# Splitting the first eight tile loads between the SyncE and ScalarE DMA queues in a cross-attention kernel

## The chip, the cores and the metric

One core of one Trainium2 chip. The metric is the device time of one launch in microseconds (us), as the median over several executions; a profiled execution gives the trace.

## The reference

Thirty-two sequences, each with 512 tokens of `x` and 512 tokens of a context, 512 features in float32, go through one cross-attention layer with 16 heads of 32 features:

```python
def layer_norm(x, gamma, beta, eps=1e-05):
    mu = jnp.mean(x, axis=-1, keepdims=True)
    var = jnp.var(x, axis=-1, keepdims=True)
    return (x - mu) * jax.lax.rsqrt(var + eps) * gamma + beta
qn = layer_norm(q, q_norm_g, q_norm_b)          # q is x
kvn = layer_norm(kv, kv_norm_g, kv_norm_b)      # kv is the context
Q, K, V = qn @ Wq, kvn @ Wk, kvn @ Wv           # split into 16 heads
attn = softmax(Q K^T / sqrt(32))
out = q + gelu((attn @ V) @ Wo + bo)            # exact gelu
```

## The kernel before

**Work.** A token tile is 128 tokens by 512 features in float32 (256 KB). A batch is one sequence: four tiles of `x` (tiles 0 to 3) and four of the context (tiles 4 to 7), all kept in the buffer `tok`. A batch is computed in four steps of four heads each. TensorE makes the products; to keep float32 precision from the fast float32r products, most operands are split into a high part (written by ScalarE) and a low part (written by VectorE), and three products of parts are summed. VectorE finds the row maxima of the scores, ScalarE takes the exponentials, GpSimd adds the probabilities up. The order of the work on each engine is written out by hand in the table `ORDER`, and the engines are held together by semaphores. The loop runs the batches -1 (which only prepares batch 0), 0, 1 to 30 in a hardware loop, 31 and 32 (which only finishes batch 31).

**The head of the kernel**, on which the change bears, is batch -1:

- SyncE (SP) issues eight tile loads of batch 0 with `load_tile` (L387 to L392), then the four weights Wq, Wk, Wv, Wo of 1 MB each into `probs` (L385), and after that the copies of the stacked operands (L353), which wait for VectorE. Later it loads the tiles of each next batch and the residuals, and stores the result.
- ScalarE (ACT) begins with five small DMAs: four of 2 KB each that bring the two layer norms' gains and offsets into `norm_rows` (L511), and one for the output's bias (L513). Then it loads its table and waits for the first tile to be normalised (L584). It copies each transposed tile out of PSUM (L588) and later makes the high parts of the weights (L525 to L537).
- TensorE (PE) waits for the four `norm_rows` DMAs together and turns them into columns (L782). Its next work is to transpose the normalised tiles (L943), with the bias rows (L788) between them.
- VectorE (DVE) makes two small masks from the identity, then waits for that transpose and copies it into `norm_cols` (L634), and only after that begins with the layer norm of the tiles: statistics (L725), their mean and variance (L731), and two small steps (L736, L737). It writes the low parts of the transposed tiles (L686).
- GpSimd (POOL) takes the power that gives the reciprocal deviation (L491, L494), and after the last tile's it scales Wq (L459).

The first items of VectorE's stream, in its order:

```python
dve.wait_ge(cols_mm, 1)
dve.tensor_copy(norm_cols[:], score[3][:, 0:4 * NC].rearrange("p (n c) -> p n c", c=NC)).then_inc(cols_ready, 1)
```

and of TensorE's:

```python
pe.wait_ge(consts, 8)
pe.wait_ge(cols_loaded, 16 * 4)
```

Of the kernel before, what the change touches and what calls it, by code (L numbers as in the profile page):

```python
# [14 lines left out]
NC = D // P  # L15
# [117 lines left out]
def plan_of(b):  # L133

    return PLAN_OF_HEAD if isinstance(b, int) and b == -1 else PLAN_OF_ALL
# [43 lines left out]
def build(nc, x, ctx_in, q_g, q_b, kv_g, kv_b, wq, wk, wv, wo, bo, out):  # L179
    B = x.shape[0]  # L180
    with ExitStack() as es:
        def sb(name, shape, dt=F32):
            return es.enter_context(nc.sbuf_tensor(name, shape, dt))
# [4 lines left out]
        def sem(name):  # L188
            return es.enter_context(nc.semaphore(name))
# [12 lines left out]
        tok = sb("tok", [P, 2 * NC, D])  # L202
# [55 lines left out]
        tile_loaded = [sem(f"tile_loaded{i}") for i in range(8)]  # L258
# [27 lines left out]
        x_v = x.rearrange("b (i p) d -> (b i) p d", p=P)  # L286
        c_v = ctx_in.rearrange("b (i p) d -> (b i) p d", p=P)
        out_v = out.rearrange("b (i p) d -> (b i) p d", p=P)

        def known(b):  # L290
            return isinstance(b, int)
# [5 lines left out]
        def valid(b):  # L297
            return not known(b) or 0 <= b < B

        def wait(eng, s, value):  # L300

            assert known(value) or value.min_val > 0
            if not known(value) or value > 0:
                eng.wait_ge(s, value)

        def last(b):
            return known(b) and b == B - 1
# [9 lines left out]
        def unit(b, s, off):  # L317

            return b + (s + off) // NU, (s + off) % NU
# [31 lines left out]
        def restack(eng, u, nat, stack, parts, done):  # L351
            for third, part in parts:
                eng.dma_start(raw(stack[DH * third:DH * (third + 1), u % 2, :, :]),  # L353
                              raw(nat[:, part, :])).then_inc(done, 16)
# [12 lines left out]
        def all_batches(eng, batch):  # L367

            batch(-1)
            batch(0)  # L370
            with eng.Fori(1, B - 1) as b:
                batch(b)
            batch(B - 1)
            batch(B)
# [4 lines left out]
        @block.sync  # L379
        def _(sp):  # L380
            def prepare(b, s):

                if (b, s) == (-1, 1):
                    for n, (name, w) in enumerate((("q", wq), ("k", wk), ("v", wv), ("o", wo))):
                        sp.dma_start(probs[:, n], w.rearrange("(c p) n -> p c n", p=P)).then_inc(w_loaded[name], 16)  # L385

            def load_tile(b, i):  # L387

                if valid(b - 1):
                    wait(sp, full["x"], 8 * (b - 1) + i + 1)  # L390
                src = x_v[NC * b + i] if i < NC else c_v[NC * b + i - NC]
                sp.dma_start(tok[:, i, :], src).then_inc(tile_loaded[i], 16)  # L392

            def load_residual(b, i):
                if last(b):
                    wait(sp, full["x"], 8 * (B - 1) + i + 1)
                    sp.dma_start(tok[:, i, :], x_v[NC * b + i]).then_inc(tile_loaded[i], 16)
                    return
                wait(sp, stored[i % 2], 16 * (2 * b + i // 2))
                sp.dma_start(res[:, i % 2, :], x_v[NC * b + i]).then_inc(res_loaded[i % 2], 16)  # L400

            def batch(b):
                PLAN = plan_of(b)
                for s in range(NU):
                    if known(b):
                        prepare(b, s)
                    b1, u1 = unit(b, s, 1)
                    b2, u2 = unit(b, s, 2)
                    for kind, n, part in PLAN["sp"][s]:
                        if kind == "load" and valid(b + 1):  # L410
                            load_tile(b + 1, n)
                        if kind in ("rq", "rk") and valid(b2) and not (kind == "rq" and known(b) and (b, s) == (-1, 2)):
                            which = kind[1]
                            wait(sp, free[which], NU * b2 + u2 + 1)
                            wait(sp, stack_used, NU * b2 + u2 + 1)
                            if which == "q":
                                restack(sp, u2, q_nat, q_stack, ((0, 0), (1, 0), (2, 1)), q_stacked)
                            else:
                                restack(sp, u2, k_nat, k_stack, ((0, 0), (1, 1), (2, 0)), k_stacked)
                        if kind == "res" and valid(b - 1) and not last(b - 1):  # L420
                            load_residual(b - 1, 2 + n)
                        if kind == "first_res" and valid(b):
                            load_residual(b, n)
                            if last(b):
                                load_residual(b, n + 2)
                        if kind == "store" and valid(b - 1):
                            wait(sp, act_out_free, 4 * (b - 1) + n + 2)
                            src = tok[:, n, :] if last(b - 1) else res[:, n % 2, :]
                            sp.dma_start(out_v[NC * (b - 1) + n], src).then_inc(stored[n % 2], 16)

            all_batches(sp, batch)
            for i in range(2):
                sp.wait_ge(stored[i], 16 * 2 * B)
# [73 lines left out]

        @block.scalar
        def _(act):
            for n, col in enumerate((q_g, q_b, kv_g, kv_b)):  # L510
                act.dma_start(norm_rows[NC * n:NC * (n + 1), :],  # L511
                              col.rearrange("(c p) -> c p", p=P)).then_inc(cols_loaded, 16)
# [479 lines left out]
```

## Time and profile before

| what | value |
|---|---|
| median of 3 runs | 3280.11 us (3278.88 to 3282.63) |
| the profiled execution | 3279.69 us |
| its span, from the first to the last instruction | 3277.9 us |
| mean granted TensorE clock | 0.998 of full speed |
| TensorE busy | 3244.4 us, 99% of the span |
| VectorE, ScalarE, GpSimd busy | 69%, 69%, 71% |
| DMA traffic | 340.15 MB, mean 104 GB/s |

A row of the chain of work gives a start, a length and what was done in it. A row of the timeline gives a start, a length, the engine (SPq and ACTq are the engines' own work of issuing DMAs), the line and the operation, and in brackets the engine's idle time before it with what ended it. Queue q1 of the DMA rows carries what SyncE issues, queue q10 what ScalarE issues. "Packets" there are single pieces of at most one row of 2 KB; the completion signals are counted among those under 512 B.

### The profile page before, as it was taken

To read this page: it belongs to the slowest core of one execution; us is meant where nothing else is said; L and a number is where in the kernel's file an instruction comes from. 1 tells how busy PE (TensorE), PEld (TensorE's weight loads), DVE (VectorE), ACT (ScalarE), POOL (GpSimd) and SP (SyncE) were. 2 spreads that over 40 slices of the span, in tenths; PEclk is the share of its full clock that TensorE was granted. 3 is DMA by queue.
4 is the path that set the end of the run, shared out by engine and by line. 5 is a ranking of instruction groups with operands and counts; after the bars stand their busy time and mean duration, and the time that the engine had idled before them with its cause. 6 is when DMAs were issued, how large, how long until landed. Compare 5 with 4: busy or idle time off the path is not lost.

```text
span 3277.9 us, 60424 instructions
## 1 busy us (share of the span) xinstructions
PE 3244.4 (99%) x16611; PEld 2140.0 (65%) x16611; DVE 2256.6 (69%) x4769; ACT 2276.0 (69%) x3985; POOL 2315.9 (71%) x1544
## 2 busy tenths in 40 slices
PE   8999999999999999999999999999999999999998
PEld 5566666666666666666666666666666666666664
DVE  6667667676676676666766766766667667667664
ACT  5677666777767777667767667776777676677765
POOL 3676776777677767777776677777767776777665
PEclk9999999999999999999999999999999999999999
DMA  6655656566556556565665566565656655666653
GB/s 142 89 106 106 107 103 113 90 108 106 105 102 103 108 106 105 103 116 87 110 107 103 105 100 109 107 102 103 119 83 111 106 106 106 98 109 106 103 78 76
DMA packets 186492, 340.15 MB, mean 104 GB/s; under 512 B 20561, under 2 KB 20577, under 8 KB 186466
## 3 DMA queue, kind: packets, MB, share of 16 engines
q1 hardware_dynamic: 186000, 339.03, 60.2%
q10 hardware_dynamic: 466, 0.80, 0.2%
q8 instruction: 13, 0.21, 0.0%
q14 instruction: 13, 0.11, 0.0%
HBM read 104.87 MB, written 33.55 MB: 42 GB/s over the span
## 4 chain that ended last, share of the span: by engine, by line
PE 97%; DVE 1%; ACT 1%; issue 1%; DMA 0%; POOL 0%; SPq 0%; ACTq 0%; POOLq 0%; DVEq 0%
PE gen L856 43%; PE score L883 15%; PE score L876 15%; PE ctx L903 14%; PE gen L847 4%; PE gen L943 4%; PE gen L965 1%; DVE maxes L706 0%; DMA k_stack<-k_nat 0%; ACT q_stack L617 0%; PE score L788 0%; DVE stats L725 0%; ACT probs L563 0%; PE gen L837 0%; POOL probs L475 0%
## 5 line engine op out<-in xcount | busy, mean ns | idle before, releaser
L475 POOL TENSOR_TENSOR probs<-probs 128x1024 f32<-128x1024 f32 x762 | 1802.0, 2396 | 291.9 <-PE ctx L903 285.7
L706 DVE TENSOR_REDUCE maxes<-score 128x1 f32<-128x512 f32 x2048 | 1295.8, 682 | 202.8 <-PE score L883 201.9
L563 ACT ACTIVATE probs<-score 128x512 f32<-128x512 f32 x2048 | 1086.3, 621 | 140.5 <-PE score L876 134.4
L883 PE MATMUL score<-k_stack,q_stack 96*128 96x512 f32 x2048 | 762.1, 413 | 3.4 <-DVE maxes L706 1.8
L876 PE MATMUL score<-q_stack,k_stack 128*128 128x512 f32 x2048 | 697.8, 407 | 6.3 <-ACT q_stack L617 6.3
L883 PEld LDWEIGHTS score<-k_stack,q_stack 96*128 96x128 f32 x2048 | 378.9, 189 | 217.6 <-ACT probs L563 83.9
L876 PEld LDWEIGHTS score<-q_stack,k_stack 128*128 128x128 f32 x2048 | 374.5, 189 | 200.8 <-DVE maxes L706 59.3
L903 PE MATMUL ctx<-probs,v_sb 128*32 128x512 f32 x4096 | 492.6, 599 | 0.0
L856 PE MATMUL gen<-w_v,cT 128*128 128x512 f32 x1536 | 462.2, 396 | 0.0
L856 PE MATMUL gen<-cT,w_k 128*128 128x512 f32 x1536 | 461.9, 400 | 0.2 <-DVE q_nat L688 0.2
L856 PE MATMUL gen<-xT,w_q 128*128 128x512 f32 x1536 | 448.6, 394 | 3.0 <-issue 0.4
L856 PE MATMUL gen<-w_o,ctx_hl 128*128 128x512 f32 x1488 | 416.3, 397 | 0.0
L491 POOL TENSOR_TENSOR rstd<-var_eps,minus_half 128x1 f32<-128x1 f32 x256 | 140.6, 549 | 343.7 <-DVE neg_mean L737 341.5
L502 POOL TENSOR_TENSOR ctx_hl<-ctx_n,ctx_hl 128x512 fp32r<-128x512 f32 x128 | 164.3, 1283 | 287.7 <-ACT ctx_hl L569 278.2
L617 ACT ACTIVATE q_stack<-max_hl,chunk_mask 32x512 fp32r<-32x512 f32 x512 | 326.3, 706 | 50.3 <-DVE max_hl L771 49.5
L856 PEld LDWEIGHTS gen<-w_v,cT 128*128 128x128 f32 x1536 | 287.7, 189 | 85.6 <-issue 26.7
L856 PEld LDWEIGHTS gen<-xT,w_q 128*128 128x128 f32 x1536 | 286.9, 189 | 68.4 <-issue 8.4
L856 PEld LDWEIGHTS gen<-cT,w_k 128*128 128x128 f32 x1536 | 287.8, 192 | 56.8 <-DVE q_nat L688 1.1
L856 PEld LDWEIGHTS gen<-w_o,ctx_hl 128*128 128x128 f32 x1488 | 277.2, 190 | 57.0
L688 DVE SCALAR_TENSOR_TENSOR k_nat<-gen,bias_k,k_nat 128x512 fp32r<-128x512 f32 x128 | 95.8, 749 | 316.9 <-ACT k_nat L608 316.9
L903 PEld LDWEIGHTS ctx<-probs,v_sb 128*32 128x32 f32 x4096 | 107.4, 109 | 236.0 <-issue 236.0
L574 ACT ACTIVATE v_sb<-gen 128x512 f32<-128x512 f32 x128 | 76.6, 598 | 257.0 <-PE gen L856 257.0
(89 smaller groups left out, 2765.7 us busy)
## 6 DMA issues: line engine op xcount, KB each, us to landing
k_stack<-k_nat SPq DMA_DIRECT2D x384, 256.0 KB, 7.8
q_stack<-q_nat SPq DMA_DIRECT2D x381, 256.0 KB, 5.6
tok<-in_x SPq DMA_DIRECT2D x132, 256.0 KB, 10.4
tok<-in_ctx SPq DMA_DIRECT2D x128, 256.0 KB, 11.0
res<-in_x SPq DMA_DIRECT2D x124, 256.0 KB, 2.6
out<-res SPq DMA_DIRECT2D x124, 256.0 KB, 2.1
probs<-in_L_xattn_Wq SPq DMA_DIRECT2D x1, 1024.0 KB, 8.1
probs<-in_L_xattn_Wk SPq DMA_DIRECT2D x1, 1024.0 KB, 10.4
```

What stands on the lines that cost most here:

```text
L475: pool.tensor_tensor(probs[:, c + 1, heads], probs[:, c + 1, heads], probs[:, c, heads], ALU.add).then_inc(pool_added, 1)
L491: pool.tensor_tensor(rstd[:, n:n + 1], var_eps[:, n:n + 1], minus_half[:], ALU.pow).then_inc(ln_rstd, 1)
L502: pool.tensor_tensor(ctx_hl[:, 1, up], ctx_n[:], raw(ctx_hl[:, 0, up]), ALU.subtract).then_inc(ctx_split, 1)
L563: act.activation(probs[:, n, part, :], score_at(s, "st", i)[:], ACT.Exp, scale=SCALE).then_inc(exp_done, 1)
L617: act.activation(q_stack[SROW:P, u1 % 2, :, P * n:P * (n + 1)], raw(max_hl[SROW:P, :]).unsqueeze(1).to_broadcast([SHIFTS, HU, P]), ACT.Ide ...
L706: dve.tensor_reduce(maxes[:, u1 % 2, SROW + i:SROW + i + 1], score_at(s, "s", i)[:], AX_X, ALU.max, negate=True).then_inc(max_done, 1)
L847: mm = pe.matmul(bank[DH * j:DH * (j + 1), :], ones[:, 0:DH], probs[:, c, j, :], start=(i == 0), stop=(i == len(chunks) - 1))
L856: mm = pe.matmul(bank[:, :], stationary(hs, c), moving(hm, c), start=(i == 0), stop=(i == len(TERMS) * NC - 1))
L876: pe.matmul(score_bank(pe, b, s, "st", i)[:, :], k_stack[:, s % 2, part, P * n:P * (n + 1)], q_stack[:, s % 2, part, :], start=True, stop= ...
L883: pe.matmul(score_bank(pe, b, s, "s", i)[:, :], q_stack[0:KROWS, u1 % 2, n, P * part:P * (part + 1)], k_stack[0:KROWS, u1 % 2, n, :], star ...
L903: mm = pe.matmul(ctx_ps[DH * j:DH * (j + 1), :], v_sb[:, c, lo:lo + DH], probs[:, c, j, :], start=(c == 0), stop=(c == NC - 1))
L943: mm = pe.matmul(bank[:, P * c:P * (c + 1)], tok[:, n, P * c:P * (c + 1)], ident[:], start=True, stop=True, is_transpose=True)
```

## The change

Of the eight tile loads of batch 0, SyncE issues tiles 0, 2, 4 and 6. Tiles 1, 3, 5 and 7 are issued by ScalarE, as the first instructions of its stream, ahead of its five small DMAs. The semaphores that the loads raise are the same. The loads of all later batches stay on SyncE.

```diff
             def load_tile(b, i):
 
+                if known(b) and b == 0 and i % 2 == 1:
+                    return
                 if valid(b - 1):
                     wait(sp, full["x"], 8 * (b - 1) + i + 1)
                 src = x_v[NC * b + i] if i < NC else c_v[NC * b + i - NC]
...
         @block.scalar
         def _(act):
+            for i in range(1, 2 * NC, 2):
+                act.dma_start(tok[:, i, :], x_v[i] if i < NC else c_v[i - NC]).then_inc(tile_loaded[i], 16)
             for n, col in enumerate((q_g, q_b, kv_g, kv_b)):
                 act.dma_start(norm_rows[NC * n:NC * (n + 1), :],
                               col.rearrange("(c p) -> c p", p=P)).then_inc(cols_loaded, 16)
```

## Rows read from the trace of the kernel before

**Rows 1.** The page: the chain that ended last, by engine

```profile
PE 97%; DVE 1%; ACT 1%; issue 1%; DMA 0%; POOL 0%; SPq 0%; ACTq 0%; POOLq 0%; DVEq 0%
```

**Rows 2.** The chain in order of time, 0 to 60 us

```profile
1.98 3.15 DMA norm_rows<-in_L_xattn_kv_norm_b
...
5.26 0.27 PE score L782
5.55 0.17 DVE norm_cols L634
5.73 0.60 DVE stats L725
...
12.17 2.82 PE gen L943 x12
...
29.73 2.94 PE gen L856 x12
...
36.14 7.21 PE gen L856 x24
```

**Rows 3.** VectorE, 0 to 20 us: its two longest waits of five

```profile
DVE cT L686 <- ACT cT L588: 2.5, 2, 1.6
DVE norm_cols L634 <- PE score L782: 2.3, 1, 2.3
```

**Rows 4.** Line L392 alone, tile 7's issue: its start, and time to landing

```profile
L392 SPq DMA_DIRECT2D tok<-in_ctx x1: 432/432/432, 4.1 to 4.1; - x1
...
DMA to landing us min/median/max: 5.9/5.9/5.9
```

**Rows 5.** Timeline of issues, with ScalarE's table load and GpSimd's first scaling of Wq

```profile
0.74 1.90 SPq L392 DMA_DIRECT2D tok<-in_x  x4
...
1.63 0.32 ACTq L511 DMA_DIRECT2D norm_rows<-in_L_xattn_kv_norm_g  x1
...
2.62 1.28 ACT L584 ACT_TABLE_LOAD   x1 [2.62 <-issue]
...
4.62 0.43 SPq L385 DMA_DIRECT2D probs<-in_L_xattn_Wq  x1
5.10 0.52 SPq L385 DMA_DIRECT2D probs<-in_L_xattn_Wk  x1
...
7.16 2.33 SPq L385 DMA_DIRECT2D probs<-in_L_xattn_Wo  x1
...
14.58 8.05 POOL L459 TENSOR_SCALAR v_sb<-probs,norm_cols 128x512 f32<-128x512 f32 x4
```

**Rows 6.** The weights' DMAs: KB each, us from issue to landing

```profile
probs<-in_L_xattn_Wq SPq DMA_DIRECT2D x1, 1024.0 KB, 8.1
probs<-in_L_xattn_Wk SPq DMA_DIRECT2D x1, 1024.0 KB, 10.4
...
probs<-in_L_xattn_Wo SPq DMA_DIRECT2D x1, 1024.0 KB, 14.2
```

**Rows 7.** SyncE's own waits, 0 to 60 us

```profile
SPq L353 <- DVE k_nat L688: 25.5, 1, 25.5
```

**Rows 8.** Two stages; busy us of PE, PEld, DVE, ACT, POOL; clock; DMA share; GB/s

```profile
4.00:9.60 5.60, 0.82 (x4) 0.74 (x5) 3.97 (x22) 1.29 (x2) 1.98 (x5) 1.00 0.96 291
9.60:19.90 10.30, 9.24 (x34) 4.50 (x33) 7.10 (x27) 8.44 (x14) 8.99 (x14) 1.00 1.04 389
```

**Rows 9.** DMA packets in 3.0 to 3.5 us, of all queues

```profile
DMA packets 83, 0.17 MB, mean 340 GB/s; under 512 B 0, under 2 KB 0, under 8 KB 83
```

**Rows 10.** DMA packets in 2.8 to 3.0 us, of all queues and of q10

```profile
DMA packets 50, 0.06 MB, mean 318 GB/s; under 512 B 16, under 2 KB 20, under 8 KB 50
...
q10 hardware_dynamic: 8, 0.00, 4.5%
```

**Rows 11.** DMA packets in 3.5 to 3.7 us, of all queues and of q1

```profile
DMA packets 39, 0.04 MB, mean 185 GB/s; under 512 B 18, under 2 KB 22, under 8 KB 39
...
q1 hardware_dynamic: 31, 0.03, 102.7%
```

**Rows 12.** A half-microsecond stretch near 38 us (columns as in rows 8)

```profile
37.50:38.00 0.50, 0.50 (x3) 0.40 (x2) 0.50 (x2) 0.50 (x2) 0.00 (x0) 0.50 1.09 119
```

## The prediction

> **What bounds the kernel now.** I read the page first. TensorE is busy for 99% of the span (the table above) and makes up 97% of the chain that ended last [rows 1], so over the 32 batches nothing that a few DMA issues do can matter, except by moving the start of TensorE's work. The change touches only the first microseconds, so I then read the chain in order of time from 0 [rows 2]. The reader is to see that it does not begin with the tiles. It begins with ScalarE's small DMAs: the fourth one (kv_norm_b) is issued at 1.98 us and lands 3.15 us later, TensorE turns the rows at 5.26, VectorE copies norm_cols at 5.55, and from 5.73 VectorE works without a pause through the layer norms and the first low part, which lets TensorE go on at 12.17. From there the chain is TensorE's. Third, the waits of VectorE [rows 3]: in 20 us it has five kinds, for ScalarE (two), TensorE's transpose, GpSimd's constants and the start of the program, and none for a tile. Its last idle time before the layer norms is the 2.3 us for norm_cols [rows 3], and a tile that landed earlier would shorten nothing. Tile 7 is not even in by then (issue just after 4.1 us plus 5.9 gives 10.05 [rows 4]), but its statistics come late in VectorE's order, and are not waited for either.
>
> So the quantity that decides is the landing of kv_norm_b, the last of the four small DMAs. I call d the time by which it lands later (or earlier). VectorE, TensorE, ScalarE and GpSimd all start behind it in a fixed order, and what is late by d at 5.55 us is late by d at 12.17.
>
> **The change, part by part.**
>
> *SyncE issues four tiles fewer.* Four took 1.90 us [rows 5], so Wq's issue moves from 4.62 to about 2.7 and the rest with it. Worth nothing: Wq lands at 4.62 + 8.1 = 12.7 [rows 5, 6], while GpSimd's first work on it is at 14.58 [rows 5], behind VectorE's and GpSimd's layer norm work; and the weights' data pass behind the same 2 MB of tiles in any case. SyncE's next instruction waits 25.5 us for VectorE [rows 7], so its free time goes into that wait. If that cover were gone, it would be worth 1.9 us.
>
> *The tile loads themselves.* The same 2 MB have to pass the same DMA engines, which are busy at a share of 0.96 from 4 to 9.6 us [rows 8]. Two issuers may let the first megabyte start up to a microsecond earlier, and no engine waits for it: zero.
>
> *ScalarE issues four tiles first.* Here is the cost. Bare issue time: four tile issues take about 1.9 us by SyncE's row [rows 5], so kv_norm_b is issued at about 3.9 in place of 1.98. ScalarE's table load (1.28 us) moves from 2.62 [rows 5] to about 4.6 and ends near 5.9. Its first tile work needs statistics that begin at 5.73 even in the kernel before [rows 2] and at least 1.9 us later here, so the load is hidden by that; without that cover it would cost its 1.28 us. If the small DMA then still took 3.15 us, d would be 1.9. This is the lower bound; nothing in the trace suggests a gain, as kv_norm_b can't be issued earlier.
>
> But it no longer travels alone. In the kernel before, queue q10 held only small DMAs beside SyncE's tiles on q1. Even so they did not slip in freely. Between 3.0 and 3.5 us 83 tile pieces pass and not one small one [rows 9], though the third small DMA had been issued by 1.95 [rows 5]. The small ones pass in bursts, at 2.8 to 3.0 and at 3.5 to 3.7, each with the completion signals of a tile: of 16 and 18 pieces under 512 B only 4 are the small DMA's own [rows 10, 11] (8 pieces of q10 in each burst, in the second as 39 less q1's 31: four of data and four signals). I read this as one small DMA for each 256 KB tile that passes, not one for each 2 KB piece. After the change the small DMAs stand behind tiles 1, 3, 5 and 7 in ScalarE's own queue, and the other queue has the tiles 0, 2, 4, 6 and then the weights. So they wait first until all eight tiles are through, 10.05 us [rows 4], and then they take turns with Wq and what follows. At 389 GB/s [rows 8], a turn as large as a tile takes 262 KB / 389 = 0.67 us, and four small DMAs take four turns: 2.7 us. kv_norm_b lands at 12.75, and d = 12.75 - 5.13 = 7.6 us. Upper bound: a turn is a whole weight DMA, so that the fourth small one passes behind Wo, which lands at 7.16 + 14.2 = 21.4 [rows 5, 6]: d = 16. Between the bounds of 1.9 and 16 I take 7.6, because the turn of 256 KB is the one that the bursts show, and the 1 MB turn has no row.
>
> The Trainium skill (DMA: Bandwidth & Descriptors, Queues, rings and completion order) says that each DMA engine goes round robin between queue rows and drains a whole packet, typically 9 to 17 descriptors and at most 64, before it switches. By that rule, the trace agrees as far as tiles go: 128 rows over 16 engines and a completion signal are 9. As an estimate from that page: with 17 a turn would be twice as long and d about 10; with a weight's 32 rows and signal in one packet, the upper bound holds.
>
> *What else is behind it.* The bias DMA lands later still and is wanted only after the products of 36.14 to 43.35 [rows 2]. Nothing absorbs d: VectorE had no wait between 5.73 and 12.17 [rows 2, 3] that would shrink, and the later waits at the head are for engines that are late by the same d. TensorE's clock can move the sum a little: the granted clock is 0.50 at 37.5 to 38 [rows 12], which is 1.2 in place of 2.4 GHz, after 32 products of one column each, and the 24 products from 36.14 took 7.21 us against 2 x 2.94 at full clock [rows 2], 1.3 us lost. Where that falls relative to the work may change: plus or minus 1.3.
>
> Sum: 0 + 0 + 7.6, so 3279.69 + 7.6 = 3287.3 for an execution like the profiled one. The median of the runs lies 0.42 above that execution, so I give 3287.7. The bound of what a measurement here can tell is 0.2%, 6.6 us: slower begins at 3286.7, and the forecast lies just past it.
>
> **The rivals.**
>
> *The small DMAs take turns piece by piece, or go ahead of the weights* (not slower). They wait for tiles 1, 3, 5, 7 in their queue, and then pass at once. For: pieces of 2 KB could be mixed freely, and two issuers may get the tiles through sooner than 10.05, since 291 GB/s there is well under 389 [rows 8]. Against: the stretch without a small piece [rows 9]. kv_norm_b lands by 10.2 at the latest, d = 5.1; with the tiles at 389 GB/s they are through 1.8 us sooner (2.1 MB/291 less 2.1 MB/389), d = 3.3. Time 3283.4 to 3285.2. It decides where the fourth small DMA lands before 5.13 + 6.6 = 11.7 us. Chance 0.3. The forecast itself with the tiles through a microsecond earlier is also inside 0.2%: of its chance of 0.36 I put 0.1 there.
>
> *The small DMAs sit behind whole weights* (slower). For: Wq is one DMA of 1 MB, and the trace shows turns as long as a DMA. By order of arrival alone, Wq and Wk (issued from 2.7 to 3.7) would be ahead of the fourth small one (3.9), and Wk lands at 5.10 + 10.4 = 15.5 [rows 5, 6]: d = 10.4. In strict turns of whole DMAs d = 16. Time 3290 to 3296. Chance 0.24.
>
> *Only the issue time counts* (same): d = 1.9, 3282. For it: the small ones go to few DMA engines, which might be less busy. Against: their own queue is in order, with tiles ahead. Chance 0.06.
>
> The Trainium skill (DMA: Bandwidth & Descriptors, Issuing engines are not separate DMA queues) says that issuing from several engines saves only the issuer's time. By that, the change could at best give the 1.9 us above, 3278.2.
>
> *Faster*: Wq early would have to matter, and it lands ahead of its use already; 0.02, for noise as well. *The change does nothing* (3280.1): the guard holds for batch 0 only and the four issues are really there, so only if ScalarE's queue were served so that kv_norm_b still landed near 5.1: 0.02.
>
> **How the numbers follow.** Forecast 0.36, behind whole weights 0.24, piece by piece 0.3, issue only 0.06, nothing 0.02, faster 0.02. Slower: 0.26 + 0.24 = 0.5. Same: 0.1 + 0.3 + 0.06 + 0.02 = 0.48. Faster 0.02. The range goes from 3283.0, the lower end of the piece by piece case with a little of the clock, to 3296.3, the upper bound; it leaves out the issue-only case and those below. The likeliest case's own range is 3286 to 3290.
>
> **What would show it.** Right: in the changed chain kv_norm_b is issued near 3.9 and lands near 12.7; norm_cols near 13.1; TensorE's L943 x12 near 19.8; VectorE waits for nothing but norm_cols (near 10 us in place of 2.3); the shift at 50 us is the same d. The piece by piece rival shows a landing by 10.2; whole weights show one past 15. Wrong altogether: a landing near 7, or a shift at 12 us that has gone by 50.

## The result, and the profile after

| | before | after |
|---|---|---|
| median of 20 runs each | 3280.56 us (3277.47 to 3284.62) | 3285.89 us (3282.51 to 3289.64) |
| span of the profiled execution | 3277.9 us | 3284.2 us |

The changed kernel is 5.33 us slower; the ratio is 1.0015, with a 95% interval of 1.0009 to 1.0020. That is inside the 0.2% that I had called no change, and it is clear of noise all the same, since 20 runs resolve more than I had assumed. (Here and below a ratio and its interval are drawn from all executions of a kernel, so the ratio differs a little from the quotient of the two medians.) The forecast was 3287.7, with a range of 3283.0 to 3296.3.

The chain of the changed kernel in order of time, 0 to 60 us (lines lie two to four further on than before: L513 issues ScalarE's tiles, L515 the small DMAs, L786 turns the rows, L638 copies the columns, L947 transposes tiles, L860 are the products):

```profile
0.73 0.42 ACTq L513
...
2.63 0.64 ACTq L515
...
3.94 6.02 DMA norm_rows<-in_L_xattn_kv_norm_b
9.96 0.14 issue
10.09 0.27 PE score L786
10.39 0.17 DVE norm_cols L638
10.56 0.60 DVE stats L729
...
17.00 2.82 PE gen L947 x12
...
35.20 2.94 PE gen L860 x12
38.14 3.46 PE score L819 x32
41.61 5.61 PE gen L860 x24
```

Beside [rows 2] three things are to be seen. The fourth small DMA is issued 1.96 us later and takes 6.02 in place of 3.15, so it lands at 9.96 in place of 5.13: d = 4.83. VectorE's statistics start 4.83 later (10.56 against 5.73), and TensorE's run of twelve transposes 4.83 later (17.00 against 12.17). Nothing absorbs it up to there. And the 24 products that took 7.21 us in [rows 2] take 5.61 here: the granted clock of this execution is 1.00 all the way to 60 us. That is why the shift at 50 us, which I had forecast to be the same d, is smaller in this pair of traces: VectorE's run of maxima starts at 54.01 against 50.14, 3.87 later.

The waits of VectorE in the changed kernel, 0 to 20 us (us in total, times, longest), against [rows 3]:

```profile
DVE norm_cols L638 <- PE score L786: 7.2, 1, 7.2
DVE chunk_mask L633 <- POOL low_row L453: 1.5, 1, 1.5
DVE maxes L630 <- PEq L985: 0.9, 1, 0.9
DVE xT L690 <- ACT xT L592: 0.7, 2, 0.5
```

The wait for the columns has grown from 2.3 to 7.2 us, and again there is none for a tile.

The stage rows (PE, PEld, DVE, ACT, POOL, clock, DMA share, GB/s) against [rows 8]:

```profile
4.00:9.60 5.60, 0.00 (x0) 0.00 (x0) 0.00 (x0) 1.28 (x1) 0.00 (x0) 1.00 1.03 367
9.60:19.90 10.30, 5.22 (x22) 4.11 (x23) 8.77 (x44) 6.58 (x11) 6.15 (x17) 1.00 0.92 344
```

From 4 to 9.6 us no engine computes anything; ScalarE's 1.28 us is its table load. All the same the data move faster than before, 367 against 291 GB/s, and they do it where nobody waits. The last section comes back to how much of that belongs to the split.

The DMA pieces of the changed kernel from 0 to 7.5 us, and then from 7.5 to 9.6 us, all queues and the two by themselves:

```profile
DMA packets 1100, 2.03 MB, mean 271 GB/s; under 512 B 108, under 2 KB 108, under 8 KB 1100
...
q1 hardware_dynamic: 581, 1.07, 42.1%
q10 hardware_dynamic: 519, 0.96, 35.2%
...
DMA packets 406, 0.73 MB, mean 348 GB/s; under 512 B 37, under 2 KB 53, under 8 KB 406
...
q1 hardware_dynamic: 315, 0.64, 89.5%
q10 hardware_dynamic: 91, 0.09, 13.3%
```

By 7.5 us the two queues have been served nearly alike. SyncE's four tiles are 4 x 144 = 576 pieces, so its queue has just come to Wq; ScalarE's lacks 57 pieces of its own 576. In the next 2.1 us those 57 and the 34 small pieces pass, while 315 pieces of the other queue do.

### The profile page after: what moved, and what is told of

It is laid out like the page before. It is cut to its first block, busy times and chain, and to the rows that moved or that the text cites. A ratio compares the mean times of both kernels' runs of the same rounds, so it can differ in the third digit from the quotient of the medians.

```text
span 3284.2 us, 60424 instructions
## 1 busy us (share of the span) xinstructions
PE 3246.8 (99%) x16611; PEld 2138.2 (65%) x16611; DVE 2255.8 (69%) x4769; ACT 2277.3 (69%) x3985; POOL 2318.4 (71%) x1544
## 4 chain that ended last, share of the span: by engine, by line
PE 97%; DVE 1%; issue 1%; DMA 1%; ACT 0%; POOL 0%; ACTq 0%; SPq 0%; POOLq 0%; DVEq 0%
PE gen L860 43%; PE score L887 15%; PE score L880 15%; PE ctx L907 14%; PE gen L851 4%; PE gen L947 4%; PE gen L969 1%; DVE maxes L710 0%; DMA k_stack<-k_nat 0%; PE score L792 0%; DVE stats L729 0%; DMA norm_rows<-in_L_xattn_kv_norm_b 0%; ACT q_stack L621 0%; POOL probs L477 0%; PE gen L841 0%
## 5 line engine op out<-in xcount | busy, mean ns | idle before, releaser
L860 PE MATMUL gen<-w_v,cT 128*128 128x512 f32 x1536 | 462.1, 396 | 0.0
L860 PE MATMUL gen<-cT,w_k 128*128 128x512 f32 x1536 | 460.6, 399 | 0.2 <-DVE q_nat L692 0.2
L860 PE MATMUL gen<-xT,w_q 128*128 128x512 f32 x1536 | 449.3, 395 | 2.5 <-issue 0.3
L860 PE MATMUL gen<-w_o,ctx_hl 128*128 128x512 f32 x1488 | 416.6, 396 | 0.0
L860 PEld LDWEIGHTS gen<-w_v,cT 128*128 128x128 f32 x1536 | 287.4, 189 | 85.9 <-issue 26.8
L860 PEld LDWEIGHTS gen<-xT,w_q 128*128 128x128 f32 x1536 | 287.4, 189 | 69.1 <-issue 7.9
L860 PEld LDWEIGHTS gen<-cT,w_k 128*128 128x128 f32 x1536 | 286.6, 192 | 57.1 <-DVE q_nat L692 1.1
L860 PEld LDWEIGHTS gen<-w_o,ctx_hl 128*128 128x128 f32 x1488 | 276.8, 189 | 56.8
L692 DVE SCALAR_TENSOR_TENSOR q_nat<-gen,bias_q,q_nat 128x512 fp32r<-128x512 f32 x128 | 95.5, 746 | 232.7 <-ACT q_nat L598 232.7
```

Of the source, the lines that this page charges most:

```text
L692: dve.scalar_tensor_tensor(out=dst, in0=psum, scalar=bias, in1=raw(hi), op0=ALU.add, op1=ALU.subtract).then_inc(done, 1)
L860: mm = pe.matmul(bank[:, :], stationary(hs, c), moving(hm, c), start=(i == 0), stop=(i == len(TERMS) * NC - 1))
```

## The experiments

Landing means the landing of kv_norm_b; "start" is the start of the twelve transposes that the chain shows at 12.17 us in the kernel before. The kernels that were executed only once are read by these two numbers alone, since totals of single executions of one kernel differ by 7 us.

**Both kernels once more.** Nothing is edited.

> The kernel before, once more, to see how far the landing varies by itself. If the landing of kv_norm_b is a property of the order of the DMAs: 5.1 us within 0.5, and L947 x12's counterpart (L943 x12) at 12.2 within 0.5. If the slow passage of the tiles (1.1 thousand pieces by 9 us, against 1.3 thousand in the kernel with the small DMAs issued late) belongs to that order too, it comes back here; if it was chance, some 1.25 thousand pieces pass by 9 us.

> The changed kernel, once more. The same DMAs in the same order landed kv_norm_b at 9.96 and, with only VectorE's copy moved, at 9.20. Theory: the landing is 9.2 to 10.2 in each execution, d between 4.1 and 5.1. If it lands at 11 or more, or below 8.5, the shares that I take from single traces (issue, own queue, weights) can't be told apart.

The chain of each, first of the kernel before, then of the changed one:

```profile
1.98 3.27 DMA norm_rows<-in_L_xattn_kv_norm_b
...
12.29 2.82 PE gen L943 x12
```

```profile
3.90 6.30 DMA norm_rows<-in_L_xattn_kv_norm_b
...
17.25 2.82 PE gen L947 x12
```

Landings at 5.25 and 10.20, starts at 12.29 and 17.25. Between these two executions of each kernel the landing repeats within 0.25 us, and d is 4.8 to 5.0. Kernels below that issue the same DMAs in the same order, with only VectorE's copy moved, landed at 4.51 and 9.20, so the landing varies by more than that, up to 1.0 us. The slower passage of the tiles in the kernel before repeats here too, 1143 pieces by 9 us against 1129 in the first trace; but the kernel that landed at 4.51 passed 1237, so it does not belong to the order of the DMAs alone. In the second execution of the changed kernel the 24 products took 7.22 us, as in [rows 2], and the shift at 50 us is then 5.50 us (55.23 against 49.73): where the low clock falls changes from one execution to the next.

In the kernels in which VectorE's copy stays at the front and the columns are what it waits for last, the start follows the landing at a fixed distance: 5.13 to 12.17 and 5.25 to 12.29 (before), 9.96 to 17.00 and 10.20 to 17.25 (changed), and, from the experiments below, 6.72 to 13.76, 7.92 to 14.97 and 8.80 to 15.84. The distance is 7.04 or 7.05 us in all seven traces.

**The copy later: where the loss goes through.** In the changed kernel VectorE waits for the columns after its sixth statistics, not before the first. (The expectations below say "seventh"; in the traces the copy stands between the sixth and the seventh.)

```diff
-            dve.wait_ge(cols_mm, 1)
-            dve.tensor_copy(norm_cols[:], score[3][:, 0:4 * NC].rearrange("p (n c) -> p n c", c=NC)).then_inc(cols_ready, 1)
...
             def prepare(b, s):
+                if (b, s) == (-1, 1):      # called ahead of the items of this step
+                    dve.wait_ge(cols_mm, 1)
+                    dve.tensor_copy(norm_cols[:], score[3][:, 0:4 * NC].rearrange("p (n c) -> p n c", c=NC)).then_inc(cols_ready, 1)
```

> The changed kernel, but VectorE waits for norm_cols only after its seventh statistics instead of before the first. Theory V (the whole loss goes through VectorE's wait): VectorE starts on tile 0 near 4.1 us, has the seven statistics done near 9.6, waits for norm_cols until 10.4, and L947 x12 starts near 11.6 to 12.2 in place of 17.0; time 3280 within 2 us. Rival (TensorE's or GpSimd's wait for the columns matters by itself): the time stays above 3284.

```profile
3.93 5.27 DMA norm_rows<-in_L_xattn_kv_norm_b
9.20 0.14 issue
9.34 0.26 PE score L789
9.59 1.06 PE gen L950 x4
...
10.67 0.61 ACT xT L592
...
11.30 0.70 DVE xT L691
...
12.05 2.74 PE gen L950 x12
```

That is its chain. The start is 12.05, ahead of the kernel before, although the small DMA still lands at 9.20. Five microseconds are won back, without touching any DMA: the way from the landing to the start has shrunk from 7.04 to 2.85 us, which is 4.2 us of them, and the remaining 0.8 is only that the columns landed earlier in this execution. The median of 11 runs is 3281.88 (3279.31 to 3287.94) beside 3280.50 for the kernel before, ratio 1.0005 (0.9996 to 1.0014): not to be told from no change. The theory holds for the 4.2 us; with a landing at 9.96 or 10.20 the same chain would start at 12.8 to 13.1, past the range that I gave. What remains of the chain shows the rival's part too: TensorE, which waits for the small DMAs ahead of everything, is now the engine that goes on from the landing. The landing is 0.8 to 1.0 us earlier than in the two executions of the changed kernel, with the same DMAs; why, I can't say, and it bounds how finely the shares below can be read.

**The small DMAs later, the tiles left alone.** The kernel before; ScalarE waits for the constants, at 2.6 us, before it issues.

```diff
+            act.wait_ge(consts, 8)
             for n, col in enumerate((q_g, q_b, kv_g, kv_b)):
```

> The kernel before (all tiles on SyncE), but ScalarE waits for GpSimd's constants, at about 2.6 us, before its small DMAs, so that kv_norm_b is issued near 3.9 with nothing ahead of it in its own queue. Theory I (issue time plus 3.15 us): landing at 7.0, d = 1.9. Theory A (the DMA engines serve in order of arrival across queues): behind tiles 0 to 6, landing at 8.5 to 9.3. Theory F (the queues share fairly in small turns, and only a queue's own backlog counts): landing at 5.5 to 6.5.

```profile
3.90 4.02 DMA norm_rows<-in_L_xattn_kv_norm_b
7.92 0.14 issue
...
14.97 2.82 PE gen L944 x12
```

Landing at 7.92, d = 2.8, start at 14.97. It lies between the three theories and bears none of them out: the DMA is issued 1.92 us later, and from issue to landing it takes 0.87 us more than the 3.15 us before, which I put down to the backlog of SyncE's tiles. Service in order of arrival would have cost more, fair service in small turns less.

**The weights held back.** The changed kernel; SyncE issues the weights only when the small DMAs are in.

```diff
                 if (b, s) == (-1, 1):
+                    sp.wait_ge(cols_loaded, 16 * 4)
                     for n, (name, w) in enumerate((("q", wq), ("k", wk), ("v", wv), ("o", wo))):
```

> The changed kernel, but SyncE waits for the four small DMAs before it issues the weights, so that nothing but the eight tiles is moved ahead of them. Theory M (the tiles in ScalarE's queue share the DMA engines with Wq, which is why they and the small DMAs were through only near 9.6): 2.1 MB at 390 GB/s from 1.9 us end at 7.3, kv_norm_b lands near 7.8, d = 2.7. Rival (the small DMAs' own chain in ScalarE's queue takes that long): landing stays at 9.5 to 10.

```profile
3.93 4.87 DMA norm_rows<-in_L_xattn_kv_norm_b
8.80 0.14 issue
...
15.84 2.82 PE gen L948 x12
```

Landing at 8.80. The direction is theory M's, and the size is not: without any weight in the way only 1.2 to 1.4 us of the changed kernel's landing go (9.96 and 10.20), and 3.7 of d stay. Even that share is not much larger than the unexplained 0.8 to 1.0 above, and beside the execution that landed at 9.20 it would be 0.4.

**Two tiles instead of four.** ScalarE issues the tiles 1 and 3 ahead, SyncE the other six.

```diff
-                if known(b) and b == 0 and i % 2 == 1:
+                if known(b) and b == 0 and i in (1, 3):
...
-            for i in range(1, 2 * NC, 2):
+            for i in (1, 3):
```

> The changed kernel with only the tiles 1 and 3 on ScalarE ahead of its small DMAs; SyncE issues the other six. Theory Q (each tile ahead costs its issue time of 0.47 us and its share of the queue): half of the changed kernel's d of 4.8 to 5.1, so kv_norm_b lands at 7.1 to 8.1. Rival (one tile ahead is as bad as four, since the small DMAs' own turns take the time): landing above 9.

```profile
2.91 3.81 DMA norm_rows<-in_L_xattn_kv_norm_b
...
13.76 2.82 PE gen L947 x12
```

Landing at 6.72, d = 1.6, start at 13.76. The issue comes 0.93 us later than before and the DMA takes 0.66 longer. The rival falls. The cost is smaller than the theory's half of d, and the landing is ahead of the expected 7.1 to 8.1: the first two tiles cost 1.6 us and the last two 3.2. A fuller queue at the time may be the reason; that is not shown.

**The small DMAs first.** ScalarE issues them first, then its four tiles.

```diff
-            for i in range(1, 2 * NC, 2):
-                act.dma_start(tok[:, i, :], x_v[i] if i < NC else c_v[i - NC]).then_inc(tile_loaded[i], 16)
             for n, col in enumerate((q_g, q_b, kv_g, kv_b)):
...
             act.dma_start(bias_all[0:1, :], bo.rearrange("(a n) -> a n", a=1)).then_inc(bo_loaded, 16)
+            for i in range(1, 2 * NC, 2):
+                act.dma_start(tok[:, i, :], x_v[i] if i < NC else c_v[i - NC]).then_inc(tile_loaded[i], 16)
```

> ScalarE issues its five small DMAs first and then the tiles 1, 3, 5, 7. Theory Q (the cost is the landing of kv_norm_b, which queued behind the four tiles in ScalarE's own queue): kv_norm_b lands at 5.1 to 5.6 us as in the kernel before, L947 x12 starts at 12.0 to 12.6, and the time is that of the kernel before, 3280.5 within 2 us. Rival W (two queues at once slow the small ones, whatever their order): landing at 8 or later, time 3283.5 or more.

The columns came in earlier than expected (TensorE turns the rows at 4.76 us), but the chain took another turn. Its row, the row that ends it, and VectorE's new waits:

```profile
3.05 6.46 DMA tok<-in_x
...
13.61 2.82 PE gen L947 x12
```

```profile
DVE norm_cols L638 <- PE score L786: 1.8, 1, 1.8
DVE stats L729 <- DMA tok<-in_x: 1.7, 2, 1.2
```

Tile 3, issued at 3.05, lands at 9.51, and VectorE waits 1.7 us for tiles, for which it waited in neither of the two kernels. The start is 13.61, 1.4 us behind the kernel before. The median of 11 runs is 3283.32 beside 3280.50, ratio 1.0006 (0.9997 to 1.0015): the interval still includes no change, though all 11 runs lie above the median of the kernel before. The expected start was missed by 1.0 us. The order of the queue decides the landing, as theory Q says; that the tiles would then be late I had not seen.

**The small DMAs first, and the weights held until the odd tiles are in.**

```diff
                 if (b, s) == (-1, 1):
+                    for i in range(1, 2 * NC, 2):
+                        sp.wait_ge(tile_loaded[i], 16)
                     for n, (name, w) in enumerate((("q", wq), ("k", wk), ("v", wv), ("o", wo))):
```

> The small DMAs first on ScalarE, then its four tiles, and SyncE holds the weights until those tiles are in. Theory W (what the small-DMAs-first kernel still lost, 1.4 us at L947 x12, is tile 3 arriving late, because ScalarE's tiles share the DMA engines with Wq): tile 3 is in by 7, VectorE waits for no tile, kv_norm_b lands at 4.6 to 5.2, and L947 x12's counterpart starts at 11.7 to 12.3. Rival (ScalarE's later issue of its tiles, from 2.6 us, is enough): it starts at 13 or later.

```profile
2.62 5.12 DMA tok<-in_x
...
13.50 2.82 PE gen L949 x12
```

Theory W falls. The start is 13.50, as good as unchanged; now tile 1, issued at 2.62 and in at 7.74, is what VectorE waits for (1.4 us). ScalarE's tiles are late with or without the weights. In the kernel before SyncE issued tile 1 at about 1.2 us and it landed 3.7 us later; here it is issued 1.4 us later and takes 5.12 us. So half of its delay is the later issue behind the five small DMAs, and the other half, the slower passage without any weight in the way, stays open.

**A version to beat both.** The kernel before with the later copy, and the same with the small DMAs issued late as well (the two edits shown above).

> The kernel before, with VectorE's wait for norm_cols moved behind its seventh statistics. Theory V (VectorE's wait is what the head of the kernel hangs on, also in the kernel before): VectorE starts on tile 0 at 3.4 in place of 5.7, is then held by the tiles' landing (tile 6 at 9.4), and L943 x12 starts near 11.3, 0.9 us earlier; time 3279.7. Rival: the tiles' landing takes all of it back, 3280.5.

> The kernel before with both: the small DMAs issued only after GpSimd's constants (2.6 us), and VectorE's wait for norm_cols behind its seventh statistics. The tiles go first and pass faster (tile 6 in near 8), kv_norm_b lands near 7.9, before VectorE asks for it near 9. Theory V: L943 x12 starts at 9.7 to 10.2, 2.0 to 2.5 us earlier than in the kernel before; time 3278.3. Rival (TensorE, which waits for the small DMAs before anything else, becomes the bound): L943 x12 at 11 or later, time 3279.5 or more.

From the chain of each:

```profile
2.68 5.39 DMA tok<-in_ctx
...
11.24 2.82 PE gen L946 x12
```

```profile
3.89 4.53 DMA norm_rows<-in_L_xattn_kv_norm_b
8.42 0.14 issue
8.56 0.26 PE score L786
...
11.27 2.82 PE gen L947 x12
```

The first starts its twelve transposes at 11.24, 0.93 us earlier than the kernel before and within 0.1 of what was expected. Its chain now begins with a tile, number 4, issued at 2.68 and in at 8.07: with the copy out of the way the tiles' landing has become what the head waits for. Its median of 11 runs is 3278.95 beside 3279.47, ratio 1.0000 (0.9991 to 1.0009): a gain of a microsecond is in the trace and can't be confirmed in the times. The second started them at 11.27, not at 9.7 to 10.2: the small DMA lands at 8.42, TensorE turns the rows only then, and its first tile waits behind them. The rival was right about the bound. Its time was 3280.94, ratio 1.0006 (0.9997 to 1.0015), no better than the kernel before. Its start follows the landing by 2.85 us, as in the changed kernel with the later copy: TensorE's own wait for the rows is the way that is left.

## Why the prediction was right and wrong

- **The path** was right. The kernel's head hangs on kv_norm_b, through TensorE's rows and VectorE's copy, and not on a tile. The chain, the growth of one wait from 2.3 to 7.2 us, the 7.04 us between landing and start in seven traces, and the later copy, which cuts that distance to 2.85, show it.
- **The terms at zero** were right: the faster tiles (367 against 291 GB/s) and SyncE's freed time bring nothing, and the table load costs nothing. What the weights cost on their way past the small DMAs belongs to the queueing term. GpSimd's first work on Wq moved with everything else, from 14.58 to 19.41.
- **The issue time** was right: 3.94 and 3.90 us against a forecast 3.9.
- **The queueing term was mis-sized**, and it is the step that failed: "they wait first until all eight tiles are through, 10.05 us, and then they take turns with Wq", four turns of 0.67 us. Landing 12.75 was forecast, 9.96 and 10.20 were measured; d was 4.8 to 5.0 in place of 7.6. The miss of 2.8 us has two parts. The last of the eight tiles, tile 7, issued by ScalarE at 2.15, landed 7.2 us later, at 9.35 and not at 10.05:

```profile
DMA to landing us min/median/max: 7.2/7.2/7.2
```

That is 0.7. The fourth small DMA landed 0.6 us behind it, and 0.75 in the second execution, where four turns of a tile would have been 2.7; that is the other 2.1. In pieces: four turns of a tile's 9 on 16 DMA engines would have let some 576 of the other queue pass, and from the end of SyncE's tiles to 9.6 us some 320 did, while ScalarE's last 57 tile pieces passed as well. With the copy moved, the fourth small DMA landed at 9.20, ahead of tile 7 at about 9.45: it does not even wait for the whole of the tile before it.

So the turns are shorter than the ones that I had read out of the bursts in [rows 9 to 11]. There the small DMAs came alone and early; the same bursts fit a small DMA that reached the DMA engines just after a tile that had been issued before it, and I had let one reading of them decide. The fourth small DMA of the kernel before, the one that matters, passed in no burst at all: of queue q10, 2 pieces passed from 3.7 to 4.0 us, 2 from 4.0 to 4.5 and 6 from 4.5 to 5.2 (two of them the bias's), between 191 pieces of tiles. That row was there to be read.
- **The rival that pieces mix freely** is the one that came true in size: d up to 5.1 and a landing by 10.2, at 0.3, against measured landings of 9.96 and 10.20 and starts 4.8 to 5.0 later. The median moved by 5.33 and lies at 3285.89, between this rival's 3283.4 to 3285.2 and the likeliest case's 3286 to 3290, in neither. That the stated range of 3283.0 to 3296.3 held it is owed to the rival, which set its lower end. Its premise is only half shown. Service was near equal while both queues were full, but neither order of arrival nor fair small turns gives the 7.92 of the kernel with late small DMAs.
- **The parts of d**, by single traces: 1.9 us of issue time, 0.9 from SyncE's backlog (7.92 less 5.13 and the issue time), 0.9 from ScalarE's own tiles ahead (8.80 less 7.92), and 1.2 to 1.4 from the weights. Only the issue time is firm. The step from 7.92 to 8.80 compares kernels that differ both in the queue of four tiles and in the weights, and kernels with the same DMAs landed at 5.13, 5.25 and 4.51, at 7.92 and 8.42, and at 9.96, 10.20 and 9.20, which is as much as the parts themselves. What one DMA engine does between two queues stays open.
- **No absorption** was right, and the clock term as well: the shift at 50 us was 3.87 and 5.50 in the two pairs of traces, d with more or less of the low clock in it; the same 24 products took 5.61 or 7.2 us in different executions, 1.6 against the forecast 1.3. Four transposes at 21.6 us took 1.05 us in the first trace of the changed kernel and 0.59 in the second; kernels with all tiles on SyncE show both values too (1.05 at 19.59 us in the one with late small DMAs), so it is not of the change.
- **The chances** leaned on the wrong side of 0.2% by a hair: 0.5 for slower, 0.48 for no change, and the median came out 0.16% slower.

## What to carry to other kernels

Before an issue is moved to another engine's queue, look at what that queue already carries and who waits for it: four 2 KB loads decided this kernel's head, and four tiles put in front of them cost 5.3 us in the medians, of which the bare issue time was 1.9. A tile that lands earlier is worth no more than the wait for it in the trace, here none. Where a small early DMA feeds a wait at the front of a busy engine's stream, move the wait behind the work that doesn't need it: that cut the way from landing to start from 7.04 to 2.85 us. It did not end it, since TensorE's own wait for the rows stayed at the front, and in the kernel before with the later copy a tile's landing has taken its place.

## What had not been expected of the hardware

The same eight tiles passed at quite different rates, and not only between kernels. By 7.5 us 864 pieces had passed in the kernel before and 1100 in the changed one, which looks like the gain of a second queue. The kernel with the small DMAs issued late, which keeps all tiles on one queue, reached 1055, which looks like the gain of taking the small DMAs out of the first tiles. But with only VectorE's copy moved, the kernel before reached 977, and the one with late small DMAs 913. The three lines are of late small DMAs, of late small DMAs with the later copy, and of the kernel before with the later copy:

```profile
DMA packets 1055, 1.88 MB, mean 251 GB/s; under 512 B 124, under 2 KB 140, under 8 KB 1055
...
DMA packets 913, 1.64 MB, mean 219 GB/s; under 512 B 102, under 2 KB 113, under 8 KB 913
...
DMA packets 977, 1.75 MB, mean 233 GB/s; under 512 B 113, under 2 KB 129, under 8 KB 977
```

So one queue with early small DMAs gave 864, 876 and 977, and with late ones 1055 and 913: the two overlap, and no effect of the small DMAs on the tiles can be read from them. The kernels with four tiles on each queue, ahead of the small DMAs, gave 1100, 1092, 1129 and 1112, all above every trace with one queue. The split did speed up the first two megabytes. Whether by the second queue itself or by the earlier issue of the tiles (the last one at 2.15 in place of 4.1 us) was not tried apart, and why one queue varies from 864 to 1055 stays open.
